# Sparse-expert FFN plus quantised FFN on one core: h turned by DMA from step 4 on, and a reordered start and end of the walk

## What is computed

```python
g = silu(einsum('bsd,fd->bsf', xn, ctx[e]))      # xn = layernorm(x)
u = einsum('bsd,fd->bsf', xn, ctx[e])            # the same product
y = einsum('bsf,df->bsd', g * u, ctx[e])
x = x + tanh(g_xattn) * (y of the token's expert)
f = silu(x2n @ fp8(gate_w) * gate_scale) * (x2n @ fp8(up_w) * up_scale)    # x2n = layernorm(x)
x = x + tanh(g_ffn) * (f @ fp8(down_w)) * down_scale
```

## Time and profile before

| | before |
|---|---|
| runs, us | 400.94, 401.18, 401.9 |
| profiled execution, us | 401.0 |
| its span, us | 399.3 |
| mean granted clock of TensorE | 0.994 of full |
| PE busy | 378.4 us (95%) |
| DVE, ACT, POOL busy | 224.1, 185.5, 163.2 us |
| all DMA engines | 75 GB/s in the mean |

### The profile page before, as it was taken

One profiled execution on the slowest core, in us unless ns is written; L12 is line 12 of the kernel. 1 busy time (PEld: TensorE's weight loads), 2 busy tenths in 40 slices (PEclk: granted clock), 3 DMA queues, 4 the chain that ended last, 5 costly groups with the idle time before them and its releaser, 6 DMA issues.

```text
span 399.3 us, 6082 instructions
## 1 busy us (share of the span) xinstructions
PE 378.4 (95%) x1920; PEld 184.3 (46%) x1920; DVE 224.1 (56%) x467; ACT 185.5 (46%) x297; POOL 163.2 (41%) x204
## 2 busy tenths in 40 slices
PE   3889899999999999999999999999999999999992
PEld 2444455555545544444444444444444444444460
DVE  5878979998787696787434222224222225322253
ACT  3779457789778428693432222222222222222220
POOL 4778889999999831411008000006200004400003
PEclk9999999999999999999999999999999999999997
DMA  7698684354445340760002000001100000200002
GB/s 263 190 313 183 127 214 113 88 108 114 101 115 112 80 105 2 178 167 0 0 2 79 28 0 0 2 0 54 53 0 0 0 0 28 79 0 2 0 0 105
DMA packets 40075, 29.99 MB, mean 75 GB/s; under 512 B 31192, under 2 KB 31216, under 8 KB 40048
## 3 DMA queue, kind: packets, MB, share of 16 engines
q1 hardware_dynamic: 37488, 21.26, 21.4%
q0 software_dynamic: 2560, 8.39, 6.1%
HBM read 18.11 MB, written 4.19 MB: 56 GB/s over the span
## 4 chain that ended last, share of the span: by engine, by line
PE 79%; DVE 10%; ACT 3%; issue 3%; POOL 2%; DMA 1%; SPq 1%; DVEq 0%; ACTq 0%; POOLq 0%
PE bank L1551 36%; PE bank L1565 17%; PE bank L1467 11%; PE bank L1483 7%; PE bank L1391 3%; PE bank L1487 3%; PE bank L1425 1%; DMA X<-x2rows 1%; DVE xs L1112 1%; DVE stats L1062 1%; DVE W L1278 1%; DVE xs L1372 1%; DVE row_hot L997 1%; DVE X L1369 1%; DVE cs L1289 1%
## 5 line engine op out<-in xcount | busy, mean ns | idle before, releaser
L1551 PE MATMUL bank<-X,W 128*128 (+1 forms) x752 | 170.0, 379 | 0.1
L1551 PEld LDWEIGHTS bank<-X,W 128*128 128x128 bf16 x752 | 73.5, 98 | 88.8 <-ACT late_norms L879 0.6
L1289 DVE SCALAR_TENSOR_TENSOR cs<-bank,up_mul,cs 128x512 f32<-128x512 f32 x47 | 35.3, 751 | 107.1 <-PE bank L1551 102.4
L1565 PE MATMUL bank<-W,cs 128*128 128x512 bf16 x376 | 89.0, 379 | 0.5 <-ACT W L762 0.5
L837 ACT ACTIVATE cs<-bank,gate_mul 128x512 f32<-128x512 f32 x47 | 32.2, 684 | 75.5 <-PE bank L1551 75.5
L844 ACT ACTIVATE cs<-cs 128x512 f16<-128x512 f32 x47 | 29.5, 628 | 79.8 <-DVE cs L1289 79.7
L676 POOL TENSOR_TENSOR xs<-xs,X 128x512 f32<-128x512 f32 x12 | 15.3, 1275 | 125.2 <-DVE X L1369 124.9
L1565 PEld LDWEIGHTS bank<-W,cs 128*128 128x128 f16 x376 | 36.6, 98 | 44.0 <-issue 0.5
L1467 PE MATMUL bank<-M,X 128*128 (+1 forms) x228 | 52.5, 379 | 2.1 <-ACT X L728 1.5
L1315 DVE TENSOR_TENSOR cs<-cs 128x512 f16<-128x512 f32 x47 | 33.7, 716 | 31.4 <-ACT cs L844 31.4
L1483 PE MATMUL bank<-M,hTh 128*128 (+1 forms) x152 | 35.9, 378 | 1.6 <-DVE xs L1112 1.6
(11 more groups left out here) (172 smaller groups left out, 385.6 us busy)
## 6 DMA issues: line engine op xcount, KB each, us to landing
ws<-in_L_ffn_gate_w SPq DMA_DIRECT2D x12, 256.0 KB, 2.6
ws<-in_L_ffn_up_w SPq DMA_DIRECT2D x12, 256.0 KB, 3.2
ws<-in_L_ffn_down_w SPq DMA_DIRECT2D x12, 256.0 KB, 2.9
cs<-in_ctx SPq DMA_DIRECT2D x2, 1024.0 KB, 6.7
X<-in_ctx SPq DMA_DIRECT2D x2, 1024.0 KB
xs<-in_x,order POOLq DMA_INDIRECT x16, 4.2
dsc<-in_L_ffn_down_scale SPq DMA_DIRECT2D x1, 256.0 KB
X<-x2rows SPq DMA_TRANSPOSE x16, 3.1
```

Source lines behind the costliest of these rows:

```text
L1289: v.scalar_tensor_tensor(out=fuse[:, c % 2, :], in0=UP[c % 2][:], scalar=up_mul[:, c:c + 1], in1=sg[:, c % 2, :], op0=ALU.mult, op1=ALU.mu ...
L1551: ins = t_.matmul(dst[c % 2][:].rearrange("p (t i) -> p t i", t=TPG), w, x2_group(g, part, k), start=(k == 0 and part == 0), stop=(k == KC ...
L1565: ins = t_.matmul(ACC[t][:], fuse_part(g, c, part)[:, t * P:(t + 1) * P], W8[:, down_slab(c), :], start=(c == 0 and part == 0), stop=(c == ...
```

## The change

- hTh and hTl become one buffer hT [P, 2, 2, KC, P] (slot, half, block, row); a second one, hrows, lies in cs.
- For steps 4 to 18 (H_DMA = 4) h isn't transposed by PE. ACT takes the high half of h from SBUF, in the step of h itself and not one later; DVE takes the low half from SBUF, behind round_stats of the same step; SP turns both halves with one DMA per step (turn_h), and PE's product_y waits for that DMA.
- SP: turn_h(s-1) stands first in step s, and the slab loads move to the step after.
- PE: word 0 of the walk (which expert a step has) is read ahead of tile 0's transposes, words 1 and 2 in steps 3 and 4. In step 2 the small transposes and the sum for expert 3's scale stand ahead of product_y(0).
- DVE: in step 2 add_expert(0) stands ahead of expert_scales, and expert_y_scales behind zh_tables.
- Behind the walk: product_y(18) behind units 1's gate and up on PE; add_expert(18) behind unit_low(0, 1) on DVE.

```diff
+    H_DMA = 4
-        hTh = sb("hTh", [P, 2, KC * P], F16)
-        hTl = sb("hTl", [P, 2, KC * P], F16)
+        hT = sb("hT", [P, 2, 2, KC, P], F16)
+        hrows = cs[:, 1, 2:4, :].bitcast(F16)
...
+        def h_turns(s):
+            return 16 * ((s - H_DMA) // 2 + 1)
...
+            def turn_h(s):
+                sp.wait_ge(y_done, s - 1)
+                sp.wait_ge(hlo_done, s + 1)
+                sp.dma_start_transpose(hT[:, s % 2].rearrange("p a k i -> p (a k) i"),
+                                       hrows[:, s % 2, :]).then_inc(hT_in[s % 2], 16)
...
             for s in range(STEPS):
+                if s > H_DMA:
+                    turn_h(s - 1)
+                if s == STEPS - 1:
+                    turn_h(s)
                 if s >= X2_LAG:
                     turn_x2(s - X2_LAG)
-                for n in slabs_of(s, s):
+                for n in slabs_of(s - 1, s - 1) if s >= 1 else ():
...
             def h_high(s, lo):
...
+                else:
+                    act.wait_ge(h_done, s + 1)
+                    if lo >= H_DMA + 2:
+                        act.wait_ge(hT_in[lo % 2], h_turns(lo - 2))
+                    a.activation(hrows[:, lo % 2, 0:D], h[:], ACT.Copy).then_inc(hhi_done, 1)
...
-                if lo >= 4:
+                if lo == H_DMA:
                     h_high(s - 1, lo - 1)
+                if lo >= H_DMA:
+                    h_high(s, lo)
...
             def h_low(s, lo):
                 dve.wait_ge(hhi_done, s + 1)
-                v.tensor_tensor(hTl[:, lo % 2, :], HT[:], hTh[:, lo % 2, :], ALU.subtract).then_inc(hlo_done, 1)
+                if lo < H_DMA:
...
+                else:
+                    v.tensor_tensor(hrows[:, lo % 2, D:2 * D], h[:], hrows[:, lo % 2, 0:D],
+                                    ALU.subtract).then_inc(hlo_done, 1)
...
-                    dve.wait_ge(hT_done, s)
+                    if lo <= H_DMA:
+                        dve.wait_ge(hT_done, s)
+                    else:
+                        dve.wait_ge(hlo_done, s)
...
                 if lo == 2:
                     round_stats(1, 1)
+                    add_expert(0)
                     expert_scales(E - 1, E)
-                    expert_y_scales(1, E - 1, E)
-                    add_expert(0)
...
-                if lo >= 2 and lo != 3:
+                if lo in (2, 4):
                     h_low(s - 1, lo - 1)
                 if lo == STEPS - 1:
                     norms_in()
+                    h_low(s, lo)
...
                     zh_tables(1, E, slice(E - 1, STEPS))
+                    expert_y_scales(1, E - 1, E)
...
                 if lo >= 4:
                     round_stats(s, lo)
+                if H_DMA <= lo < STEPS - 1:
+                    h_low(s, lo)
                 for n in slabs_of(s, lo):
...
-            add_expert(STEPS - 1)
             unit_low(0, 0)
             late_stats(1)
             unit_fuse(0, 1)
             unit_low(0, 1)
+            add_expert(STEPS - 1)
...
             pe.wait_ge(order_done, 1)
+            words = walk_words(pe)
+            load_word(t_, words, 0)
             pe.wait_ge(xn_done, 1)
...
             def product_y(s, lo):
                 e = expert_of(words, s) if lo else 0
-                pe.wait_ge(hhi_done, s + 1)
+                if lo < H_DMA:
+                    pe.wait_ge(hhi_done, s + 1)
+                else:
+                    pe.wait_ge(hT_in[lo % 2], h_turns(lo))
...
-                if lo >= 1:
-                    turn_h(s - 1, lo - 1)
+                if 1 <= lo <= H_DMA:
+                    turn_h(s - 1, lo - 1)
...
+                if lo in (3, 4):
+                    load_word(t_, words, lo - 2)
...
-            turn_h(STEPS - 1, STEPS - 1)
             x2_landed(pe, TPG - 1)
             gate_or_up(0, 0, 0)
             product_y(STEPS - 2, STEPS - 2)
             pe.wait_ge(norms_read, 1)
             gate_or_up(0, 0, 1)
+            gate_up(0, 1)
             product_y(STEPS - 1, STEPS - 1)
-            gate_up(0, 1)
             gate_up(0, 2)
```

More of the change, by code:

```diff
@@ L261, in build @@
         hT_done = sem("hT_done")
+        hT_in = [sem("hT_in0"), sem("hT_in1")]
         hhi_done = sem("hhi_done")
@@ L788, in h_high @@
             def h_high(s, lo):
-                act.wait_ge(hT_done, s + 1)
-                if lo >= 2:
-                    act.wait_ge(y_done, s - 1)
-                a.activation(hTh[:, lo % 2, :], HT[:], ACT.Copy).then_inc(hhi_done, 1)
+                if lo < H_DMA:
+                    act.wait_ge(hT_done, s + 1)
+                    if lo >= 2:
+                        act.wait_ge(y_done, s - 1)
+                    a.activation(hT[:, lo % 2, 0], HT[:].rearrange("p (k i) -> p k i", k=KC),
+                                 ACT.Copy).then_inc(hhi_done, 1)
+                else:
[3 more added lines that the diff above has]
+                    a.activation(hrows[:, lo % 2, 0:D], h[:], ACT.Copy).then_inc(hhi_done, 1)
             def step(s, lo):
@@ L880, in late_norm @@
                              ACT.Copy).then_inc(norm_read, 1)
-            h_high(STEPS - 1, STEPS - 1)
             late_abs(0)
@@ L1316, in unit_low @@
                                 ALU.subtract).then_inc(fl_done, 1)
-            h_low(STEPS - 1, STEPS - 1)
             ffn_scales(0, 0, 2)
@@ L1435, in expert_block @@
                 return M[:, ds(e, 1), part, k, :].rearrange("p a f -> p (a f)")
-            words = walk_words(pe)
             def z_operands(s, lo):
@@ L1482, in product_y @@
                     for part in range(2):
-                        t_.matmul(Y[:], hTh[:, lo % 2, k * P:(k + 1) * P], expert_block(e, part, k),
+                        t_.matmul(Y[:], hT[:, lo % 2, 0, k, :], expert_block(e, part, k),
                                   start=(k == 0 and part == 0), stop=False)
-                pe.wait_ge(hlo_done, s + 1)
+                if lo < H_DMA:
+                    pe.wait_ge(hlo_done, s + 1)
                 for k in range(KC):
-                    ins = t_.matmul(Y[:], hTl[:, lo % 2, k * P:(k + 1) * P], expert_block(e, 0, k), start=False,
+                    ins = t_.matmul(Y[:], hT[:, lo % 2, 1, k, :], expert_block(e, 0, k), start=False,
                                     stop=(k == KC - 1))
@@ L1508, in step @@
                               stop=True)
-                for n in squared_of(s - 1, lo - 1) if lo >= 1 else ():
-                    norms(n, n, n % 2, SMALL, KC * n)
-                if lo < STEPS - 1:
-                    z_next[0] = z_operands(s + 1, lo + 1)
                 if lo == 2:
@@ L1516, in step @@
                               stop=True).then_inc(msum_done, 1)
+                if lo in (2, 3):
+                    product_y(s - 2, lo - 2)
+                if 1 <= lo <= H_DMA:
+                    turn_h(s - 1, lo - 1)
+                for n in squared_of(s - 1, lo - 1) if lo >= 1 else ():
+                    norms(n, n, n % 2, SMALL, KC * n)
+                if lo in (3, 4):
+                    load_word(t_, words, lo - 2)
+                if lo < STEPS - 1:
+                    z_next[0] = z_operands(s + 1, lo + 1)
                 if lo >= 4:
@@ L1528, in norms @@
                 ins.then_inc(norm_done, 1)
-            for i in range(WORDS):
-                load_word(t_, words, i)
             z_next = [z_operands(0, 0)]
```

5 lines of the change are left out of this document (3 added, 2 removed).

## The result

| | before | after |
|---|---|---|
| median of the runs | 401.54 us (400.94 to 402.21, 4 runs) | 410.51 us (407.33 to 412.79, 4 runs) |
| ratio, 95% interval | | 1.0217 [1.0146, 1.0288] |
| profiled execution, its span | 401.0, 399.3 | 410.71, 409.0 |
| busy, whole span: PE, DVE, POOL | 95%, 56%, 41% | 92%, 56%, 41% |

The kernel became slower by 9.0 us, 2.2%. The sign was forecast, the size was not: 405.5 was expected, and 410.5 lies above the range. Ratios leave out runs more than 1.5% above the fastest of their kernel, which touches psum_loads_first (three of 12 runs) and h4_fill (two of 12) only; for these the ratio over all runs is given too.

A forecast was written before the change was run, and what follows sets the result against it. PE and POOL were both taken as full. POOL's chain (-0.9 start, +6.2 collisions, b_inv 3.95 later, +0.3 end) gave 4.25 us, SP and PE's 4.8; between them 4.5: 401.0 + 4.5 = 405.5 us, range 403 to 408.

The forecast's parts named there:

- The 6.6 us of transposes: PE in the walk: 15 groups of four transposes of h leave, 0.44 us each, 6.6 us less work.
- Collisions of h_low: DVE against POOL in the walk: 14 h_low with two SBUF inputs each cost POOL 0.44 us, 6.2 us.
- the whole h_low each time: Rival, 17 in 100: each h_low costs POOL its whole 0.69 us, 9.7 instead of 6.2 us, giving 409.0 us.
- Slab loads one step later: SP's queue: four slots are in use and a load lands well before its use, so it costs nothing.
- y(t) tied to x2_low(t-8) + 6.2 us: PE's product y through SP's queue: can't start until 6.2 us after POOL starts x2_low(t-8), so the 6.6 us become waits.
- Waits at y for the DMA, half a us a step: Sign expected in the profile after: PE waits at product y for the DMA into hT, half a us a step.
- The landing of 3.1 us: SP's transposing DMA of h: lands 3.1 us (up to 4.2) after its start.
- The start: Earlier word read and reorder in step 2: advance DVE and POOL by 0 to 1.9 us, taken as 0.9.
- The end of the walk: add_expert(18) behind the low half of fuse(0,1) on DVE: first down product 0.3 us later.

The follow-up runs named there:

- psum_loads_first: The changed kernel with h of steps 5 to 18 kept in PSUM and slab loads ahead of turn_x2: 405.25 us, ratio 1.0046 (1.0074 over all runs).
- h4_fill: psum_loads_first with 12 filler products on PE in step 4: 405.65 us, ratio 1.0065 (1.0078 over all 12 runs).
- h_in_psum: The changed kernel with h kept in a PSUM bank from step 5 on, where h_high and h_low read it: 407.42 us, ratio 1.0143.
- psum_pool_less: h_in_psum with POOL's first instruction for each slab on 128 of 512 columns only: 400.4 us, ratio 0.9941.
- start_alone: The kernel before with only the new start (word reads moved, new order of step 2): 402.78 us, ratio 1.0011.
- fill_step4: The changed kernel with 12 filler products in step 4, ahead of the transposes of h(3): 411.11 us, ratio 1.0251.
- before_pool_less: The kernel before with POOL's first instruction for each slab on 128 of 512 columns only: 400.76 us, ratio 0.9983.

## Why the prediction was right and wrong

*The 6.6 us of transposes* leave PE: right (a step of 5.72 us where nothing waits, 5.71 forecast).

*Collisions of h_low*: right in kind, and at POOL nearly in size. I summed 14 x 0.44 = 6.2 us; POOL's instructions became 5.4 us longer than with h in PSUM, 0.38 each, its last slab came 4.9 later, and the time moved by 3.0 us, which is not clear of noise. The upper bound, 9.7 us from the whole h_low each time, was not reached. **The Trainium skill** (SBUF — State Buffer, "Who interferes with whom") has the loser wait for the whole instruction. The timeline above agrees: h_low was done 0.55 us after x2_low ended at 83.97, and ln_tab, begun at 83.93, needed about 0.5 us more than in the kernel before, while h_low ran on to 84.52. As the average of all 14 the whole instruction is nearly twice too much.

*Slab loads one step later, "nothing"*: **this is the step that failed.** I reasoned from the slots ("a load lands well before its use") and wrote that "if POOL slips a load slips with it", but priced neither. The row that gave it away was in my own picture of SP's queue: the load stands behind turn_x2, which waits for POOL. By itself the edit costs 3.3 us in the kernel before; in the kernel after, moving the loads ahead of turn_x2 brings 4.4 us in the medians (410.5 to 406.1, 1.0 ± 0.9%), about what the forecast of 4.5 fell short of the measured 9.0. In the kernel after it is the place behind turn_x2 that costs: with the loads back in their old step and still behind it, the time rises to 413.6.

*y(t) tied to x2_low(t-8) + 6.2 us*: half right. That POOL holds PE in the changed kernel is borne out: less work on POOL brings 8 us there (h_in_psum against psum_pool_less). The path is another. x2_low(9) came at 137.02 (136.1 forecast), but y(17) at 145.78 instead of 142.3, and PE waits for hT only twice, 2.1 us. What holds y is mostly add_expert: DVE works later as well. "Waits at y for the DMA, half a us a step" is wrong. The landing of 3.1 us that I took from turn_x2 has a median of 3.5 for turn_h and reaches 5.8, for the turn issued at 81.81 right behind a turn_x2 and two slab loads, and 4.8 for the first one: I read the number where the DMA engines have room.

*The start*, 0.9 us: nothing (start_alone 1.0011). PE came 1.7 us earlier to a product that waits for DVE's h(3). *The end of the walk*, +0.3: right (0.4 from b_inv to the first down product).

*TensorE's clock* was in no term. In the profile after it fell three times, each behind a wait of 1.9 to 2.4 us, and each time twelve products took 1.6 to 1.7 us longer. In the kernel before PE had no such wait in the walk. Where POOL and DVE are late this costs little (fill_step4); at y(16) it lies on the way to b_inv, 4.10 instead of 1.35 us of waiting there; once the rest was repaired one such spot cost 1.3 us with 11 turns, and with 7 turns no more than the noise.

*What bounds the kernel before*: I let POOL bound it beside PE. before_pool_less contradicts that: POOL's 21 first slab instructions at 0.46 instead of 1.27 us, 17 us less work, gave 0.2%, at the edge of the error. POOL is full without slack to give, so it passes delays on, but speeding it up brings nothing as long as PE has its old list. In the changed kernel, with h in PSUM, the same relief brings 8 us.

The loss can be put in a row by the ratios of four kernels, each with one edit more, over all runs: 1.0217, 1.0116 (loads ahead of turn_x2), 1.0074 (h in PSUM), 1.0002 (11 turns). That is 4.1 + 1.7 + 2.9 = 8.7 us. The errors are 1.0 ± 0.9%, 0.4 ± 0.7% and 0.7 ± 0.5%; without the three slowest runs of the third kernel the last two are 2.8 and 1.8 us (0.7 ± 0.6%, 0.4 ± 0.4%). So the first part is shown and the other two together (4.6 us, 1.1 ± 0.6%), but not how they divide. The first is also seen from the other side, late loads alone 3.3 us in the kernel before. Of the rivals, the whole h_low each time (409.0) was nearest in time, and wrong in its cause.

What stays open: how much of the last part is the late landing of the first turn. Two profiles of slower executions (psum_loads_first, 6.45 us of waiting for it; h4_fill, 3.52) and the range of that wait, 0 to 6.45 us over the kernels with 15 turns, point to it, also for why single runs of psum_loads_first reach 400 us; no execution of psum_loads_first near 400 us was profiled, and why the landing varies so much isn't known.

## What to carry to other kernels

Before a load or a DMA is moved in an in-order queue, write down what it will wait behind and who releases that: a one-step delay that is harmless by the buffers cost more here than the new instructions did. A full engine that is not the bound still hands delays on, so price each added collision and late transfer at it. Relieving it brought nothing here while TensorE had its old list (0.2%), and 2.0% once work was taken from TensorE: a change can move the bound, and a test on the kernel before doesn't tell for the kernel after. When transposes go from TensorE to DMA, start where the DMA engines have room, keep the source in PSUM if GpSimd is busy (the collisions went with it, though the gain in time was not clear of noise), and look at the granted clock behind every new wait of TensorE of 2 us or so: it fell behind some and not behind others.

## What the runs showed of the hardware

- Behind some waits of TensorE of 1.9 us and more the granted clock was lower: in the kernel after 0.72 to 0.81 in the mean over 6 us behind waits of 2.44, 1.86 and 2.13 us, with eight products in 2.7 to 3.6 us instead of 1.89. That is the lower of its two levels, 1.2 instead of 2.4 GHz, for part of the stretch. The length of the wait does not decide it: behind 1.90 us at 126.66 in the same profile, and behind the same 2.44 us in start_alone (45.91), products ran at full speed. A wait of 1.33 us in the kernel before was followed by none. With twelve fillers in the halt the clock stayed at 1.00.
- The transposing DMA of h landed in 3.0 us at best and 5.8 at worst in the kernel after, and once in 8.6 in psum_loads_first; its issue on SP took 1.23 to 1.25 us in the kernel after.
- A DVE instruction of 0.68 us with two SBUF inputs took 1.65 to 1.78 in six of 15 cases, each time when a GpSimd instruction had begun 0.04 to 0.09 us before it. When it was itself first by 0.02 to 0.07 us, the GpSimd instruction took 1.67 to 1.79 instead of 1.16 to 1.27 (four cases). With one input in PSUM it took 0.68 to 0.69 in all 14, GpSimd being as busy (66.9 of 72 us in both kernels).
